# When the sums of gathered expert rows begin, and in what pieces the result goes out

## The reference

```python
probs = jax.nn.softmax(x @ Wr, axis=-1)
topk_w, topk_idx = jax.lax.top_k(probs, K)             # K = 2 of E = 8 experts
topk_w = topk_w / jnp.sum(topk_w, axis=-1, keepdims=True)
for i in range(E):
    w_i = jnp.sum(topk_w * (topk_idx == i), axis=-1, keepdims=True)
    h = silu(x @ Wg[i]) * (x @ Wu[i])                  # 256 -> F = 256
    output = output + w_i * (h @ Wd[i])                # 256 -> 256
```

## Time and profile before

| what | value |
|---|---|
| median of 3 runs | 713.44 us (712.94 to 714.83) |
| profiled execution, its own time | 712.27 us |
| its span | 710.5 us |
| PE busy | 639.8 us (90%) |
| DVE busy | 494.7 us (70%) |
| ACT busy | 348.2 us (49%) |
| POOL busy | 243.2 us (34%) |
| first / last tile's `gated` | 558.8 / 688.0 us |
| first / last gather issued | 648.83 / 703.76 us |
| last result issued | 707.22 us |

### The profile page before, as it was taken

How to read it: one execution, slowest core, us unless ns; L and a number is a source line. 1 busy time by engine, 2 the same in 40 slices (tenths; PEclk the granted TensorE clock), 3 DMA queues, 4 the chain that set the end, 5 groups by cost and what they waited for, 6 DMA issues and landing times.

```text
span 710.5 us, 15274 instructions
## 1 busy us (share of the span) xinstructions
PE 639.8 (90%) x5650; PEld 474.2 (67%) x5650; DVE 494.7 (70%) x1155; ACT 348.2 (49%) x1183; POOL 243.2 (34%) x219
## 2 busy tenths in 40 slices
PE   3787999998899999999999999999979899998770
PEld 2466777777787757667677766775656788887650
DVE  4988799996467878549884598736878737543562
ACT  1477799997570116601365014721277465543430
POOL 2112000000007537524377553873545000303544
PEclk9998899996899999999999999999989999999995
DMA  8799920000000000000001200011071223534454
GB/s 296 159 349 419 418 91 2 2 2 2 1 10 23 0 1 3 2 16 1 2 1 39 82 1 1 2 60 46 24 256 53 83 79 112 157 101 120 146 164 138
DMA packets 49896, 61.54 MB, mean 87 GB/s; under 512 B 15520, under 2 KB 42400, under 8 KB 49568
## 3 DMA queue, kind: packets, MB, share of 16 engines
q1 hardware_dynamic: 45088, 50.88, 21.7%
q0 software_dynamic: 3072, 8.39, 3.9%
q10 hardware_dynamic: 1664, 1.31, 0.6%
HBM read 29.37 MB, written 31.20 MB: 85 GB/s over the span
## 4 chain that ended last, share of the span: by engine, by line
PE 76%; DVE 9%; ACT 7%; issue 3%; DMA 2%; another core or an unknown queue 1%; POOL 1%; ACTq 0%; POOLq 0%; DVEq 0%
PE bank L354 65%; PE bank L363 11%; ACT kbd L1524 1%; DVE wlo L1391 1%; ACT vbd L1510 1%; DMA lncol<-in_L_attn_ln_kv_b 1%; DMA gb<-slots,index 1%; ACT ex L1534 1%; ACT xth L1490 1%; ACT ex L1649 0%; DVE m L1114 0%; DVE xhat L1350 0%; ACT wbh L1580 0%; DVE qc L1374 0%
## 5 line engine op out<-in xcount | busy, mean ns | idle before, releaser
L1114 DVE TENSOR_TENSOR m<-bank,cst 128x512 f32<-128x512 f32 x192 | 121.9, 683 | 38.5 <-PE bank L354 37.1
L1795 POOL TENSOR_TENSOR r<-m,m 128x512 f32<-128x512 f32 x80 | 104.5, 1331 | 114.7 <-DVE m L1114 95.4
L1649 ACT ACTIVATE ex<-bank,nmax 128x64 f32<-128x64 f32 x256 | 71.3, 336 | 25.2 <-DVE nmax L1357 25.2
L354 PE MATMUL bank<-xth,wbh 128*128 128x512 f32 x192 | 79.9, 416 | 1.1 <-DVE m L1114 1.1
L354 PE MATMUL bank<-xth,wbl 128*128 128x512 f32 x192 | 75.2, 392 | 0.0
L354 PE MATMUL bank<-xtl,wbh 128*128 128x512 f32 x192 | 75.1, 391 | 0.0
L1633 ACT ACTIVATE qc<-bank 128x512 f32<-128x512 f32 x32 | 17.4, 596 | 102.5 <-PE bank L354 102.5
L354 PE MATMUL bank<-wop,qc 128*128 128x256 f32 x256 | 62.5, 389 | 0.0
L354 PE MATMUL bank<-r,wqk 64*64 64x512 f32 x512 | 57.7, 594 | 0.0
L354 PEld LDWEIGHTS bank<-wop,qc 128*128 128x128 f32 x256 | 46.4, 189 | 15.1 <-issue 8.7
L1534 ACT ACTIVATE ex<-bank,nmax 128x64 f32<-128x64 f32 x256 | 54.5, 360 | 1.6 <-DVE nmax L1016 1.5
(11 more groups left out here) (217 smaller groups left out, 1482.4 us busy)
## 6 DMA issues: line engine op xcount, KB each, us to landing
slots<-cst SPq DMA_DIRECT2D x1, 13312.0 KB, 44.2
xs<-slots SPq DMA_DIRECT2D x46, 128.0 KB
slots<-ys SPq DMA_DIRECT2D x46, 128.0 KB
slots<-cst SPq DMA_DIRECT2D x1, 5120.0 KB, 49.2
wo_s<-in_L_xattn_Wo SPq DMA_DIRECT2D x1, 2048.0 KB, 17.7
wq_s<-in_L_xattn_Wq SPq DMA_DIRECT2D x1, 2048.0 KB, 12.5
wraw<-in_L_ffn_Wg SPq DMA_DIRECT2D x8, 256.0 KB, 4.6
wraw<-in_L_ffn_Wu SPq DMA_DIRECT2D x8, 256.0 KB, 4.8
```

Source lines behind the costliest of these rows:

```text
L354: return e.matmul(o, l, r, start=start, stop=stop, skip_group_check=True)
L1114: last = e.tensor_tensor(m4[n % 2][m][:, :].rearrange("p (b s) -> p b s", s=S), products[half][:, :].rearrange("p (b s) -> p b s", s=S), t ...
L1649: last = e.activation(ex[b % 4][:, h * 64:(h + 1) * 64], score_banks(b)[odd][:, n * 64:(n + 1) * 64], ACT.Exp, bias=nmax[b % 4][:, 4 * odd ...
L1795: last = e.tensor_tensor(rope[n % 6][half][:, :], m4[n % 2][first][:, :], m4[n % 2][second][:, :], op)
```

## The change

`combine(0)` moves from step 36 to step 39, and every later one with it. Steps 39 to 47 hold `combine(0)` to `combine(8)`; `combine(9)` to `combine(11)` stand behind the loop, ahead of the second part's four (`tiles + 2 - COMBINE_AT` = 9). In the loop there is one result, (0,6) in step 46, and behind it (6,12), (12,13), (13,14), (14,15) and (15,16).

```diff
-        COMBINE_AT = TILES[0] + 5
+        COMBINE_AT = TILES[0] + 8
...
-                if COMBINE_AT <= i < COMBINE_AT + 12:
+                if i >= COMBINE_AT:
                     combine(i - COMBINE_AT)
-            for t in range(12, NT):
+            for t in range(tiles + 2 - COMBINE_AT, NT):
                 combine(t)
...
-                if i in (COMBINE_AT + 6, COMBINE_AT + 10):
-                    result(i - COMBINE_AT - 6, i - COMBINE_AT - 2)
-            for lo, hi in ((8, 13), (13, 14), (14, 15), (15, 16)):
+                if i == COMBINE_AT + 7:
+                    result(0, 6)
+            for lo, hi in ((6, 12), (12, 13), (13, 14), (14, 15), (15, 16)):
                 result(lo, hi)
```

## The result

The changed kernel took 721.33 us (median of 4, 721.02 to 723.86) against 713.19 us for the kernel before on the same chip: ratio 1.0114, 95% interval 1.0085 to 1.0143. It is 8.1 us slower; forecast were 714.0 us and at most 717.0. Its profiled execution took 721.62 us with a span of 719.8, 9.3 us more than the span of before.

The account below looks back on a forecast made before the run. The kernel was taken as a chain three quarters TensorE, its last part slowed by gathers. Terms -1.35, -0.34, +1.02 and +1.2 gave +0.5 us: 712.8 us profiled, 714.0 us median; range 711.0 to 717.0.

Parts of the forecast that it names:

- (c): Drain, gated(45) to last store: gathers 18, 19 and 20 fall into it, +1.02 us, bounds 0 and 1.6.
- rival C: Slower: dense gathers beside the loop from step 39 cost 0.54 us each, +4.4 us with results, 717.8 us; chance 0.23.
- (a): Step 38 to 39: without gathers in flight 3.89 us becomes 2.54, -1.35 us, bounds 0 and -1.35.
- (b): Steps 39 to 45: ten gathers run before step 45 instead of eleven, -0.34 us, bounds 0.34 x 2 either way.
- (d): Step 46: 0.79 MB of result ahead of the last store instead of 0.52, +1.2 us, bounds +0.8 and +2.0.
- POOL's queue 1 us short of being the bound: Before gather 24: gathers 16 to 23 end at 694.5, the store releases gather 24 at about 695.5 us.
- (e): Steps 42 to 43: result(0,4) leaves the loop, taken as 0, bound -2.54 us.
- (f): Tail: result(6,12) falls among the last gathers as result(8,13) did, taken as 0, bounds -0.2 and +0.6 us.
- Steps 34 to 38: Loop steps beside the first eight gathers, which stay as before: nothing changes up to step 38.
- The model of the loss: Steps 34 to 45: 9.7 us are lost, all while POOL issues gathers; a gather costs the loop time, path unknown.

Follow-up runs that it names:

- hold_six: The changed kernel with gathers 18 to 23 held back until all 46 tiles are copied; 713.96 us, ratio 1.0031 to the kernel before.
- first_eight_paced_2: The changed kernel with all sums and result (0,6) behind the loop and gathers 0 to 7 released one a step; 720.21 us.
- results_only: The kernel before with its sums and gathers kept and only the results cut as in the changed kernel; 711.94 us, ratio 1.0015.
- before_look: The kernel before, unaltered, run again with a profile on another chip; 701.95 us.
- sums_only: The changed kernel with the results cut as in the kernel before; 714.9 us, ratio 1.005 to the kernel before.

## Why the prediction was wrong

**The step that failed is (c), the drain.** It put "gathers 18, 19 and 20 fall into it. At 0.34 us each that is +1.02 us", bounded by 1.6. Measured: +7.26 us on A, and drains of 10.2 us on B and 10.1 us on F. The reason is in the price, a mean per gather over the loop. `hold_six` shows that the gathers make it, and the semaphores show how: TensorE's completions come up to 7.65 us late. `first_eight_paced_2` shows no price at all for gathers a step apart, and on D the three gathers that (c) had counted did fall into the drain (677.19, 678.44 and 679.93) and cost nothing. What costs, on the chips with losses, is a run of gathers 1.26 us apart. Why it weighs more in the drain is our reading, not tested by itself: in the loop other tiles' work waits in TensorE's stream and takes up part of the delay; in the drain each delay of the chain TensorE, ScalarE, VectorE is paid in full. As the drain grows, more gathers fall into it, six on A in place of three. Before, the last gather was issued at 687.59, so the drain was nearly free; by moving the sums, the run was moved over it. The rival C had named density, but priced it per gather as well, and put it in the loop.

**(a) and (b)** were right in sign. Step 38 to 39 fell by 0.81 us, not 1.35: 3.3 to 3.5 us remain on chips without any loss, so only part of its excess came from gathers, and the 2.54 us taken for an undisturbed step were too low there. For the same reason the kernel before lost about 9 us to gathers on A and not 9.7: steps 34 to 45 take 28.76 us without loss, not 27.9. Steps 39 to 45 fell by 1.68 us, where -0.34 was forecast, bounds 0.68 either way; the price per gather failed there too.

**(d)** was forecast at +1.2 us with bounds 0.8 to 2.0. Measured: +1.33 (A), +0.9 (B, `results_only`), +1.84 (D). That a result ahead delays the store was right: 2.45 us with none ahead and 3.23 with 0.52 MB (D). The size on D is in part another thing: with no result ahead POOL's own queue already sets 4.31 us, and the 0.79 MB add 0.76 to that. The prediction had put POOL's queue 1 us short of being the bound; on D it was 0.8 us short, while on A gather 23 at 695.70 leaves it far off. The Trainium skill (DMA: Bandwidth & Descriptors, "Queues, rings and completion order") says that each DMA engine consumes the descriptors of a ring in order; the 2.45 against 3.23 us agree with that.

**(e), (f)** were right in size. In `before_look` the steps 41 to 42 and 42 to 43 took 2.55 us each beside result (0,4), and on B `results_only`, without that result in the loop, took 19.87 us for steps 39 to 45, no less than the 19.32 of before on A. Step 42 to 43 did fall from 5.08 to 3.08 us on A, against the forecast sign, but step 41 to 42 rose from 3.23 to 4.95 as the gathers moved. The tail changed by -0.1 us (A) and +0.4 us (D).

**Steps 34 to 38** were to stay as they were, since the program is the same there; the sum held them at nothing. On A they took 3.86 us more, with a half-speed clock. In every other trace of a kernel with these gathers on a chip with losses (B and F, and the kernel before on A) they took 14.4 to 14.5 us and the clock did not fall. All four executions of the changed kernel on A had a mean granted clock of 0.950 to 0.956, where the one on F had 0.960; so the fall may have come in each, but that is argued. Why it came on A alone is open: on F TensorE was busy 5.76 of the 9 us from 650 to 659, not much more than the 5.51 on A, and kept its clock. Without it the 8.1 us would be about 4, as on B (+3.8 us, without the results' part) and F (+3.0 us, one run each).

**The model of the loss** rested on one chip. That the lost time follows the gathers was right; that it belongs to the kernel alone was not. On C and D the kernel before is 9 to 11 us faster and its trace (D) shows no loss, and the change costs 1.0 to 1.8 us, within the 0.3%.

Open: by what path the indirect gathers hold TensorE's completions back, and what sets the chips apart. The Trainium skill (SBUF — State Buffer, "Who interferes with whom") says that a DMA never contends with a compute engine. Chips C and D agree with 2.55 us steps under back-to-back gathers. On A, B and F the steps of up to 7.8 us and the 5.3 us waits fit it badly; but whether the transfers or POOL's issuing of them makes the contact isn't shown.

## What to carry to other kernels

When work is moved off a busy loop, look at what it lands on. A delay that a full pipeline absorbs in part can be paid whole in its last steps, so a stream that disturbs it should end before them; and a mean cost per item says nothing there. A small transfer that something waits for should not be issued behind a large one that nobody waits for. And a term read from one chip's trace should be seen on a second chip before the sum leans on it.

## What the hardware showed unexpectedly

- Chips differ in how they stand back-to-back indirect gathers: the same kernel took 711 to 713 us on three and 702 us on two, and most of the difference lies in steps 34 to 45 (37.67 us on A against 28.76 on D).
- On the former, eight indirect gathers 1.26 us apart cost 4.2 us, four in the same steps, one a step, cost nothing, and eight plain transfers of the same size from the same queue, within 4.39 us, cost nothing.
- Under such gathers TensorE's semaphore rose up to 7.65 us (A), 6.84 us (B) and 5.78 us (F) behind the end of its last matmul, where 0.01 us is usual.
- The waits were nearly the same from kernel to kernel: 5.32 us (`sums_only`, chip B), 5.33 and 5.36 us (F), 5.34 us (A) ahead of the copies in the drain.
